# Experts stage of a vision tower: the full gelu goes back into the W1 product's PSUM banks, and W1's second half is issued one tile later

## The reference, cut to what matters

```python
C = 64; HID = 256; E = 8
H = gelu(xf @ W1 + b1)                    # exact gelu, fp32
probs = softmax(H @ Wg + bg)
assign = argmax(probs)
for e in range(E):
    y = H @ Wd[e] + bd[e]
    out = out + where(assign == e, probs[:, e:e+1] * y, 0)
return h + out                            # xf is the layernorm of h, rows of 64
```

## Time and profile before

| | |
|---|---|
| median of 3 runs | 679.58 us (679.23 to 679.91) |
| the profiled execution | 679.56 us, of which the span is 677.8 us |
| TensorE, matmul busy | 593.3 us, 88% |
| VectorE busy | 531.1 us, 78% |
| GpSimd busy | 410.4 us, 61% |
| ScalarE busy | 266.4 us, 39% |
| mean granted clock of TensorE | 0.943 |
| the experts stage | from about 363 us to the end |

### The profile page before, as it was taken

The page is one execution under the profiler, slowest core; times in us unless marked ns, Lnnn a source line. Parts: engine busy times, 40 slices in busy tenths (PEclk is TensorE's granted clock), DMA queues, the critical chain, the costliest instruction groups (busy, mean ns, idle before and its releaser), DMA issues. The chain is left out here.

```text
span 677.8 us, 9715 instructions
## 1 busy us (share of the span) xinstructions
PE 593.3 (88%) x2998; PEld 436.9 (64%) x2998; DVE 531.1 (78%) x966; ACT 266.4 (39%) x691; POOL 410.4 (61%) x562
## 2 busy tenths in 40 slices
PE   0699999966995799999984599999999999999994
PEld 0477777754763688778763277766666666766672
DVE  6688888873596688888871378898889988888985
ACT  2132223223473122222223765555555555555310
POOL 1689999610154043333336248888878778888777
PEclk9999999995795999999997599999999999999998
DMA  6200000000000000000000000000000000000001
GB/s 252 49 2 0 0 1 1 0 0 1 0 0 1 0 1 0 1 0 0 1 0 0 1 1 16 16 17 15 17 15 12 6 15 16 17 16 16 15 17 31
DMA packets 13140, 9.78 MB, mean 14 GB/s; under 512 B 4524, under 2 KB 12844, under 8 KB 12844
## 3 DMA queue, kind: packets, MB, share of 16 engines
q1 hardware_dynamic: 13084, 9.29, 4.3%
q10 hardware_dynamic: 16, 0.00, 0.0%
HBM read 5.10 MB, written 4.20 MB: 14 GB/s over the span
## 5 line engine op out<-in xcount | busy, mean ns | idle before, releaser
L1382 PE MATMUL ex_pE<-ex_WdP,ex_hid 128*128 128x512 f32 x774 | 203.7, 405 | 0.0
L1382 PEld LDWEIGHTS ex_pE<-ex_WdP,ex_hid 128*128 128x128 f32 x774 | 138.8, 187 | 41.7 <-issue 10.9
L1694 POOL TENSOR_TENSOR ex_s<-ex_ms 128x1024 f32<-128x1024 f32 (+1 forms) x33 | 84.3, 2554 | 46.8 <-DVE ex_ms L1525 46.8
L1525 DVE TENSOR_TENSOR ex_ms<-ex_pE,ex_gate 128x512 f32<-128x512 f32 x129 | 87.8, 682 | 22.9 <-PE ex_pE L1382 22.5
L1195 POOL TENSOR_TENSOR hT<-hT,ssm_gelu 128x512 f32<-128x512 f32 x32 | 47.7, 1508 | 94.8 <-ACT ssm_gelu L1168 94.8
L723 DVE TENSOR_TENSOR inv_prod<-inv_pW,m_img 128x504 f32<-128x504 f32 x144 | 91.7, 681 | 17.1 <-PE inv_pW L638 15.4
L649 PE MATMUL inv_pS<-ident,inv_prod 128*128 128x128 f32 x576 | 87.5, 274 | 4.7 <-DVE inv_prod L723 4.7
L649 PEld LDWEIGHTS inv_pS<-ident,inv_prod 128*128 128x128 f32 x576 | 69.8, 140 | 27.2 <-DVE inv_prod L723 19.3
L638 PE MATMUL inv_pW<-inv_ysb,m_conv2L 98*128 98x512 f32 x144 | 69.4, 485 | 2.3 <-DVE inv_ysb L711 2.3
L1446 ACT ACTIVATE ex_hidf<-ex_pH,b1c 128x512 f32<-128x512 f32 (+1 forms) x68 | 45.1, 663 | 55.9 <-PE ex_pH L1335 55.9
L1151 ACT CAST ssm_z<-ssm_back 128x512 fp32r<-128x512 f32 x32 | 18.3, 618 | 101.5 <-DVE ssm_back L1127 101.5
(11 more groups left out here) (242 smaller groups left out, 1048.3 us busy)
## 6 DMA issues: line engine op xcount, KB each, us to landing
m_img<-in_x SPq DMA_DIRECT2D x2, 2048.0 KB, 9.2
out<-ex_res SPq DMA_DIRECT2D x16, 256.0 KB, 2.2
WdT<-in_L_ffn_Wd SPq DMA_DIRECT2D x2, 256.0 KB
bd<-in_L_ffn_bd SPq DMA_DIRECT2D x16, 2.0 KB
W1d<-in_L_ffn_W SPq DMA_DIRECT2D x2, 64.0 KB
m_Bm<-in_L_attn_fwd_B_real SPq DMA_DIRECT2D x2, 16.0 KB, 2.0
m_Bm<-in_L_attn_fwd_B_imag SPq DMA_DIRECT2D x2, 16.0 KB, 2.0
m_Bm<-in_L_attn_bwd_B_real SPq DMA_DIRECT2D x2, 16.0 KB, 2.0
```

What stands on the lines that cost most here:

```text
L1382: last = nc.tensor.matmul(pE[n % 3][0:P].rearrange("p e f -> p (e f)"), hid[i % 2][value][:, h, par, 128 * j:128 * j + P], WdP[weight][:, ...
L1525: nc.vector.tensor_tensor(ms[b % NB][0:P, t % TPB, :].rearrange("p (e f) -> p e f", e=EX), pE[n % 3][0:P], gate[i % 2][0:P, t, :].unsqueez ...
L1694: nc.gpsimd.tensor_tensor(s4[0:P, 0:T], m[:, :, 0:4 * F], m[:, :, 4 * F:], ALU.add).then_inc(halved, 1)
```

## The change

Four things change.

- ScalarE's `gelu` writes the high part first and then the full gelu over its own input in pH. The tile `hidf` is gone, and so is ScalarE's wait for the parts of the item before.
- VectorE's `part` takes its first operand from pH, in PSUM, and no longer from SBUF.
- `hide` now waits for `parted` instead of `gelued`: the bank is free only when VectorE has taken the low part from it. In TensorE's window `hide(i+1, 1)` moves behind `speak(i, 2)`, `judge` behind `speak(i, 5)`, and `gates` behind `speak(i, 6)`.
- VectorE's window gets another order: `keep_bias` and the parts of the second half move back, `finish` moves ahead of `multiply(i, 3)`, `choose_best` behind `multiply(i, 6)`, and `weigh_best` behind `multiply(i, 7)`, just ahead of `normalise`.

```diff
--- before.py
+++ after.py
@@ -1240,7 +1240,6 @@
         fac = [sb(f"fac{n}", [128, 4, TPI]) for n in range(2)]
         xn = sb("xn", [128, TPI, F])
         u = [[sb(f"u{n}{t}", [128, CH], F32R) for t in range(2)] for n in range(2)]
-        hidf = sb("hidf", [128, 2, 2, CH])
         hid = [[sb(f"hid{n}{t}", [128, 2, 2, CH], F32R) for t in range(2)] for n in range(2)]
         level = sb("level", [4 * EX, CH])
         gT = sb("gT", [128, 128], F32R)
@@ -1328,7 +1327,7 @@
                 def hide(i, h):
                     pe.wait_ge(u_made, i + 1)
                     if i > 0 or h > 0:
-                        pe.wait_ge(gelued, 4 * i + 2 * h)
+                        pe.wait_ge(parted, 4 * i + 2 * h)
                     for value, weight in PARTS:
                         for par in range(2):
                             r = slice(F * par, F * par + F)
@@ -1400,26 +1399,22 @@
                     more, later, last_in = there(i + 1), there(i + 2), there(i + 4)
                     if more:
                         hide(i + 1, 0)
-                    for t in range(min(now, 2)):
+                    for t in range(min(now, 3)):
                         speak(i, t)
                     if more:
                         hide(i + 1, 1)
-                    if now > 2:
-                        speak(i, 2)
                     if now:
                         turn_gate(i)
                     if later:
                         turn_out(i + 2)
-                    for t in range(3, min(now, 5)):
+                    for t in range(3, min(now, 6)):
                         speak(i, t)
                     if more:
                         judge(i + 1)
-                    if now > 5:
-                        speak(i, 5)
+                    if now > 6:
+                        speak(i, 6)
                     if more:
                         gates(i + 1)
-                    if now > 6:
-                        speak(i, 6)
                     if now:
                         add_bias(i)
                     if last_in:
@@ -1438,13 +1433,10 @@
                 def gelu(i, h):
                     if i >= 2:
                         act.wait_ge(spoke, TPI * (i - 1))
-                    if i >= 1:
-                        act.wait_ge(parted, 4 * (i - 1) + 2 * h + 2)
                     for par in range(2):
                         act.wait_ge(hidden, 4 * i + 2 * h + par + 1)
-                        for o in (hidf, hid[i % 2][0]):
-                            last = nc.scalar.activation(o[:, h, par, 0:cols(i)], pH[par][:, 0:cols(i)], ACT.Gelu,
-                                                        bias=g.b1c[:, h:h + 1])
+                        for o in (hid[i % 2][0][:, h, par, 0:cols(i)], pH[par][:, 0:cols(i)]):
+                            last = nc.scalar.activation(o, pH[par][:, 0:cols(i)], ACT.Gelu, bias=g.b1c[:, h:h + 1])
                         last.then_inc(gelued, 1)
 
                 def keep_gate(i):
@@ -1528,7 +1520,7 @@
                 def part(i, h, par):
                     v.wait_ge(gelued, 4 * i + 2 * h + par + 1)
                     c = slice(0, cols(i))
-                    nc.vector.tensor_tensor(hid[i % 2][1][:, h, par, c], hidf[:, h, par, c], hid[i % 2][0][:, h, par, c],
+                    nc.vector.tensor_tensor(hid[i % 2][1][:, h, par, c], pH[par][:, c], hid[i % 2][0][:, h, par, c],
                                             ALU.subtract).then_inc(parted, 1)
 
                 def minus_sum(i):
@@ -1615,39 +1607,40 @@
                     more = there(i + 1)
                     if now:
                         multiply(i, 0)
-                    if there(i - 1):
-                        keep_bias(i - 1)
                     if more:
                         part(i + 1, 0, 0)
                     if now > 1:
                         multiply(i, 1)
                     if more:
                         part(i + 1, 0, 1)
+                    if there(i - 1):
+                        keep_bias(i - 1)
                     if there(i + 3):
                         minus_sum(i + 3)
                     if now > 2:
                         multiply(i, 2)
+                    if there(i - 1):
+                        finish(i - 1)
+                    if now > 3:
+                        multiply(i, 3)
                     if more:
                         part(i + 1, 1, 0)
-                        part(i + 1, 1, 1)
-                    if now > 3:
-                        multiply(i, 3)
-                    if there(i - 1):
-                        finish(i - 1)
                     if now > 4:
                         multiply(i, 4)
+                    if more:
+                        part(i + 1, 1, 1)
                     if there(i + 2):
                         low(i + 2)
                     if now > 5:
                         multiply(i, 5)
-                    if more:
-                        choose_best(i + 1)
                     if now > 6:
                         multiply(i, 6)
                     if more:
-                        weigh_best(i + 1)
+                        choose_best(i + 1)
                     if now > 7:
                         multiply(i, 7)
+                    if more:
+                        weigh_best(i + 1)
                     if there(i + 3):
                         normalise(i + 3)
```

## The result

The changed kernel takes **691.85 us** (median of 4 runs, 689.32 to 696.2) against 679.75 us for the kernel before in the same job (4 runs). The ratio is 1.0166, 95% interval 1.0084 to 1.0248. A second job with the same kernel gave 694.32 us (692.66 to 696.38), ratio 1.0199, interval 1.0161 to 1.0236. So it is slower, as forecast, but by 12 us (13 in the second job) and not by 6.5. The median lies 1.35 us above the top of my range. The profiled execution took 696.2 us, of which the span is 694.4 us.

What follows compares the result with a forecast made beforehand. It took a loop through GpSimd's tree, the factor and a blocked normalise (17.89 us a window) to bound the kernel. From 679.56 us, +1.6, +0.4, +1.0, +2.9 and +0.6 gave +6.5: 686.1 us, range 672 to 690.5.

Steps and rivals of the forecast that it cites:

- the loop: W1's second half waits for parts behind multiply 7, weigh_best, normalise; multiply 7 waits for TensorE's last tile: 18.0 us a window.
- Step 1: TensorE, from W1's second half into the next window's first tile work: multiply 7 starts at 11.70 us.
- Steps 2 to 4: After multiply 7: second tree at 0.77 us, blocked gate ends at 3.25, normalise at about 3.18, taking 0.68.
- the rival in which it comes first: GpSimd's next tree instruction gets in ahead of normalise, which waits 1.28 us in some 12.5 windows: 702 us, chance 0.13.
- Step 5: VectorE from multiply 0 through the parts: last part ends at 6.26 us, TensorE starts some 0.05 later, at 6.31.
- Window 13: A late window of the experts stage, where normalise is tiny and nothing is loaded: 17.3 us.
- the end: The last 41.25 us of the stage: the gate instruction meets the tree once more, +0.6 us.
- The start: In window -1, W1's second half will wait for two parts instead of gelu: +1.6 us.
- The rival with TensorE as the bound: Gate not held up, so TensorE's own 17.0 us bounds each window: 672.5 us, chance 0.17.
- The rule beside it: A tensor_scalar with its only tensor in SBUF can take the lock; weigh_best's first instruction blocked would delay normalise 1.3 us.

Runs made afterwards that it cites:

- part_early: The changed kernel with the last part one place earlier on VectorE, ahead of multiply 4: 690.1 us, ratio 1.0123.
- bias_first: weigh_first_part_early with add_bias ahead of gates on TensorE: 678.34 us, ratio 0.993.
- again: The changed kernel unaltered, run in a second job: 694.32 us, ratio 1.0199.
- tree_waits: The changed kernel with one more wait on GpSimd: the second tree starts only when ex_gate is written. 681.05 us, ratio 0.9983.
- weigh_first_part_early: The changed kernel with weigh_best back ahead of multiply 7 and the last part ahead of multiply 4: 678.7 us, ratio 0.9944.
- normalise_first: The changed kernel with normalise ahead of weigh_best, both behind multiply 7: 730.75 us, ratio 1.072.

## Why the prediction was wrong

The direction, the loop and its mechanism were right. The size was not, and the range missed by 1.35 us.

- **Step 1, the TensorE leg: too short, and the step that failed most.** I put multiply 7 at 11.70; it came at 525.16 in a window whose second half of W1 had begun 11.94 earlier (513.22). Two terms had been taken at nothing. Judge waits for the last part, now a place further back, which ends 5.80 us into this count and not at 5.6: part_early recovered 0.17 us. And add_bias, now directly behind the four small transposes, takes 0.34 us from its start to turn_in's (541.12 to 541.46), which I had left at the old 0.23: +0.11. In bias_first another order of these three won back 0.03 of it. The other matmuls in their new order gave back 0.07 (without judge's wait the leg to the next first half is 11.66 in part_early, against my 11.62), and multiply 7 started 0.11 and not 0.08 behind that first half.
- **Steps 2 to 4: right.** L1687 at +0.77, the gate's end at +3.25, normalise at +3.17 and 0.68 long, on the spot. L1689 asked 0.07 us after normalise and came second; the rival in which it comes first (702) did not happen.
- **Step 5: 0.1 us short.** The last part ended at +6.25 as worked out, but TensorE started at +6.39: 0.14 us from the end of VectorE's part (531.41) to the matmul (531.55), where I had written 0.05.
- **Together 11.94 + 6.39 = 18.33 and not 18.0.** Over the eleven windows from 2 to 12 (433.38 to 634.79, 201.4 us against 198.0) that is 3.4 of the missing 4.5 us.
- **Window 13** was taken at 17.3 and took 17.95. The tiny normalise stands at its end, so it shortens the wait one window later: from 641.34 to 658.82, between second halves of W1, it is 17.48 us. I had put the saving on the wrong side of the cut: +0.65 here, and the end cost 0.4 us where I had 0.6.
- **The start**: hide(0, 1) came 5.97 us after hide(0, 0), where it had been 4.25: +1.7 and not +1.6. From there to window 2 the stage took some 0.5 us more than I had given it. In `again` it took another 1.8, at the lower clock, for which the forecast had no term: with it the stage costs 13.0 us and not 11.0, and the top of my range stood at 10.9.
- **The rival with TensorE as the bound** (672.5, windows 17.0) happened where an experiment took the block away, but at 17.1 to 17.28 us a window and 678.3 to 681 us. Without the block the new order gains 0.2 to 0.7% (the 0.2 of tree_waits is not clear of noise), and not the 1% of the rival (whose sum, besides, has the start at 1.8 us where the main one has 1.6). In weigh_first_part_early, windows 2 to 13 take 204.5 us against 212.4, 7.9 less and near the 8.9 of the rival; but the stage up to window 2 takes 52.6 us against 48.5 (its window -1 is one of the long ones), and the end 42.4 against 41.25.
- **The rule beside it**, that a tensor_scalar takes part in the turns, changed nothing in the changed kernel, where it starts at 525.76, 0.17 ahead of the tree. It decided normalise_first.

The error that I had allowed, 0.1 us a window, was about the right size for each single term. But three terms had it (0.17, 0.11 and 0.08), all in the same direction, in each of some 13 windows.

## What to carry to other kernels

A wait that closes a new loop between two engines has to be summed all the way round, and every cover that is taken at nothing on the way (a part that "just arrives", a handoff of 0.05 us) is multiplied by the number of windows; better give each the largest value that its rows allow. A small instruction with two SBUF inputs, or a tensor_scalar on SBUF, should not be put on the critical path directly behind the one that releases a big GpSimd instruction: 0.2 us of work became 1.3 or 2.4 us. Where a change has a new data path and a new order, price each without the other: here either alone lost 5.6 to 6.2%, and together, with weigh_best and one part put further forward again, they gained 0.6%.

## What the runs showed of the hardware

- A wait of TensorE can cost more than its length. Behind waits of 1.15 and 1.47 us once a window the granted clock stayed at 1.00. Behind 1.86 us it fell to the lower level in every window, behind 2.47 in about every second one and behind 2.13 in 8 of 12 (0.50 to 0.68 over stretches of 2 to 5 us behind the wait), and such a window grew by a further 1.5 us or a little more. What decides between them was not tried.
- VectorE and GpSimd kept the order of asking down to 0.07 us (normalise at 528.33, L1689 at 528.40, which then took 1.76 us in place of 1.28).
- Inside one and the same GpSimd instruction (L1687, 525.93 to 528.33) VectorE's tensor_tensor with two SBUF inputs was held up (1.34 us in place of 0.23), its reciprocal was not (0.55).
- A gelu of 128x512 into PSUM is slightly shorter than into SBUF, 660 against 688 ns. The first row below is rounded on its way out and the second is not, but in the kernel before the gelu in fp32 into SBUF took 688 ns as well. Of the changed kernel, by shape:

```profile
L1439 ACT ACTIVATE ex_hid<-ex_pH,b1c 128x512 fp32r<-128x512 f32 x64 | 44.0, 688 | 83.9 <-PE ex_pH L1334 83.9
L1439 ACT ACTIVATE ex_pH<-ex_pH,b1c 128x512 f32<-128x512 f32 x64 | 42.2, 660 | 0.0
```
